# Three weight transfers issued ahead of the first rows, three more put into one run, on the queue of a state-space and LSTM kernel

## The reference, cut to what matters

```
x  = r                                   # (8 batches, 2048 steps, 512 features)
h  = layernorm(x)
y  = gelu(causal_conv(h, K) + D * h)     # K: one kernel of 2048 taps per feature, from a state-space model
x  = x + layernorm(y)
u  = layernorm(x)                        # what the LSTM-like cell reads
c0 = in_c for each of the 2048 positions
for each batch b, in order:              # u[b] is (2048 positions, 512)
    f = sigmoid(u[b] @ wf.T + c @ uf.T + bf)
    i = sigmoid(u[b] @ wi.T + c @ ui.T + bi)
    g = tanh   (u[b] @ wc.T + c @ uc.T + bc)
    c = f * c + i * g
h   = tanh(u @ wo.T + c_final @ uo.T + bo)
out = x + layernorm(h)
```

## Time and profile before

| | |
|---|---|
| median of three runs | 2647.38 us (2645.84 to 2648.0) |
| span of the profiled execution, first to last instruction | 2645.3 us |
| mean granted TensorE clock over the span | 0.983 |
| TensorE busy | 2527.1 us, 96% |
| VectorE, ScalarE, GpSimd busy | 1839.7, 1621.4, 1124.1 us |
| one core's HBM traffic | 292.88 MB read, 180.88 MB written |

### The profile page before, as it was taken

The page is one execution under the profiler, slowest core; times in us unless marked ns, Lnnn a source line. Parts: engine busy times, 40 slices in busy tenths (PEclk is TensorE's granted clock), DMA queues, the critical chain, the costliest instruction groups (busy, mean ns, idle before and its releaser), DMA issues.

```text
span 2645.3 us, 57571 instructions
## 1 busy us (share of the span) xinstructions
PE 2527.1 (96%) x22659; PEld 2205.2 (83%) x22659; DVE 1839.7 (70%) x3415; ACT 1621.4 (61%) x3003; POOL 1124.1 (42%) x1433
## 2 busy tenths in 40 slices
PE   5499999997899999999999999999999999999998
PEld 4278888886788888888888888888888888888887
DVE  7855556547887677776777887777677774467667
ACT  8657667566655555555556665555555554378777
POOL 7768687725332123222224342222222320067667
PEclk9799999998999999999999999999999999999999
DMA  8779797889774455445665755544556432489998
GB/s 348 294 227 310 266 316 268 272 292 335 195 196 116 125 141 164 127 116 125 146 161 153 193 162 142 162 130 116 124 142 159 131 85 49 156 337 347 369 360 347
DMA packets 507551, 542.52 MB, mean 205 GB/s; under 512 B 273936, under 2 KB 412944, under 8 KB 488720
## 3 DMA queue, kind: packets, MB, share of 16 engines
q1 hardware_dynamic: 507280, 538.85, 65.5%
HBM read 292.88 MB, written 180.88 MB: 179 GB/s over the span
## 4 chain that ended last, share of the span: by engine, by line
PE 84%; DVE 4%; POOL 4%; ACT 4%; DMA 2%; issue 2%; SPq 1%; DVEq 0%; POOLq 0%; ACTq 0%
PE bank L2150 31%; PE bank L2160 29%; PE bank L2206 8%; PE bank L2039 4%; PE bank L1989 3%; PE bank L2025 3%; PE bank L2047 2%; PE bank L2001 2%; PE bank L2181 2%; DVE big L1831 1%; PE bank L2009 1%; POOL big L890 1%; ACT big L1345 1%; POOL big L994 1%; DVE big L1888 1%
## 5 line engine op out<-in xcount | busy, mean ns | idle before, releaser
L2150 PE MATMUL bank<-big 128*128 128x256 f16 x8064 | 1081.2, 274 | 18.6 <-ACT big L1391 8.0
L2160 PE MATMUL bank<-big 128*128 128x256 f16 x7056 | 962.4, 273 | 0.0
L2150 PEld LDWEIGHTS bank<-big 128*128 128x128 f16 x8064 | 791.6, 98 | 116.4 <-ACT big L1391 9.7
L2160 PEld LDWEIGHTS bank<-big 128*128 128x128 f16 x7056 | 690.4, 98 | 79.9
L1035 POOL TENSOR_SCALAR big<-big 128x1 f32<-128x1 f32 x253 | 107.7, 426 | 1092.3 <-DVE big L1678 810.1
L1888 DVE TENSOR_TENSOR big<-bank,big 128x512 f32<-128x512 f32 x256 | 174.8, 683 | 196.9 <-PE bank L2160 193.8
L2206 PE MATMUL bank<-big 128*128 128x256 f16 x2688 | 295.3, 273 | 4.4 <-ACT bank L1325 4.0
L1301 ACT ACTIVATE big<-big 128x512 f32<-128x512 f32 x384 | 289.6, 803 | 14.0 <-DVE big L1888 11.9
L2206 PEld LDWEIGHTS bank<-big 128*128 128x128 f16 x2688 | 262.4, 98 | 36.9 <-ACT bank L1325 4.9
L1874 DVE TENSOR_TENSOR big<-bank,big 128x512 f32<-128x512 f32 x256 | 176.1, 688 | 142.8 <-PE bank L2160 119.1
L1233 ACT ACTIVATE big<-big 128x512 f32<-128x512 f32 x256 | 205.9, 808 | 104.4 <-POOL big L1037 101.1
(11 more groups left out here) (234 smaller groups left out, 3712.1 us busy)
## 6 DMA issues: line engine op xcount, KB each, us to landing
xtd<-big SPq DMA_DIRECT2D x60, 1024.0 KB, 6.9
big<-xr SPq DMA_DIRECT2D x16, 2048.0 KB, 9.1
big<-xg SPq DMA_DIRECT2D x64, 512.0 KB, 7.6
big<-kpad SPq DMA_DIRECT2D x32, 1024.0 KB, 12.1
yd<-big SPq DMA_DIRECT2D x16, 2048.0 KB, 16.8
big<-x SPq DMA_DIRECT2D x128, 256.0 KB, 3.3
x1d<-big SPq DMA_DIRECT2D x128, 256.0 KB, 3.2
big<-x1d SPq DMA_DIRECT2D x64, 512.0 KB, 8.8
```

What stands on the lines that cost most here:

```text
L2150: ins = e.matmul(o, WX[2 * g + lw][:, q, kt, 128 * a:128 * a + 128], slot[u % 2][:, part, lx, k0 + kt, :], start=(first and kt == 0 and (l ...
L2160: ins = e.matmul(o, WC[2 * g + lw][:, q, kt, 128 * a:128 * a + 128], cc[unit(u)[1] % 2][:, qc, lx, kt, :], start=False, stop=end, skip_gro ...
```

## The change

The definition of `load_y` is moved up unchanged, so that it can be called from the loop over turns. In turn i = NG, the last, SyncE now issues `load_y(0)`, waits for the four loads of WX[0..3] to have landed, and issues WX[4], WX[5] and WC[0]. From its old places `load_y(0)` with its wait, these three loads, and the later loads of WC[3], WC[4] and WC[5] are taken out; the last three now stand behind WC[1]. Nothing else is changed, and on no other engine is an instruction added, removed or moved.

```
                 if i == NG - 1:
                     ...
+                if i == NG:
+                    w.wait_ge(s["cv"], G * (NG - 1))
+                    load_y(0)
+                    w.wait_ge(s["wx"], 16 * 4)
+                    load_WX(4)
+                    load_WX(5)
+                    load_WC(0)
...
                     turn(8 * v + 1)
-                    load_WC(3)
                     store_x1(v, 3)
-                    load_WC(4)
...
                     store_xt(0)
-                    load_WC(5)
                     w.wait_ge(s["xs0"], 16)
                     w.wait_ge(s["xs1"], 16)
...
-            w.wait_ge(s["cv"], G * (NG - 1))
-            load_y(0)
             for c in CHUNKS[:2]:
                 load_x1(0, c)
...
-            w.wait_ge(s["wx"], 16 * 4)
-            load_WX(4)
-            load_WX(5)
             w.wait_ge(s["w_lo"], low_base(8))
             w.wait_ge(s["wd"], stored(7))
             w.wait_ge(s["fb"], 12)
-            load_WC(0)
             load_WC(1)
+            load_WC(3)
+            load_WC(4)
+            load_WC(5)
 
             w.wait_ge(s["fb"], 20)
             load_WC(2)
```

More of the change, by code:

```diff
@@ L600, in load_WC, with load_y @@
                 e.dma_start(WC[n].rearrange("p q k f -> p q (k f)"), wg[2 * g + 1][:, l]).then_inc(s["wc"], 16)
+            def load_y(v):
+                b, j = unit(v)
+                src = yd[:, :, b, 4 * j:4 * j + 4, :].rearrange("g t k h -> t g k h")
+                if v == 0:
+                    w.wait_ge(s["y0"], 16 * 7)
+                    w.wait_ge(s["y1"], 16 * 7)
+                    e.dma_start(yt[:, 0:NG - 2], src[:, 0:NG - 2]).then_inc(s["yl"], 16)
+                    return
+                w.wait_ge(s["y0"], 16 * 8)
+                w.wait_ge(s["y1"], 16 * 8)
+                if v == 1:
+                    w.wait_ge(s["yc"], 2)
+                elif v == 2:
+                    w.wait_ge(s["x1"], 4)
+                    w.wait_ge(s["yl"], 32)
+                else:
+                    w.wait_ge(s["ss"], 8 * v)
+                    w.wait_ge(s["xh"], 8 * v - 2)
+                    w.wait_ge(s["xlo"], 8 * v - 2)
+                e.dma_start(rows_y(v), src).then_inc(s["yl"], 16)
             e.dma_start(sm, small).then_inc(s["sm"], 16)
```

20 lines of the change are left out of this document (removed).

## The result

The changed kernel takes 2651.02 us (median of 20 runs, 2648.29 to 2652.72), the kernel before 2646.63 us (20 runs, 2645.09 to 2648.82). That is +4.4 us; the ratio is 1.0017, 95% interval [1.0011, 1.0023]. The forecast was 2650.7 us, or +3.3 over a kernel before of 2647.38; with 20 runs the kernel before is 0.75 us lower, so the forecast is 0.3 us off as a time and 1.1 us off as a change. The profiled execution took 2650.75 us, its span is 2649.1 us, 3.8 us more than before, at a mean granted clock of 0.982 (0.983 before).

What follows compares the result with a forecast made beforehand. The bound was TensorE, busy 96%, behind a start-up chain at 585 to 692 us whose delays reach the end one to one. 0.0 + 4.4 - 0.0 - 1.1 = +3.3 us gave 2650.7 us, range 2645.0 to 2655.0.

Steps and rivals of the forecast that it cites:

- Part 1: `load_y(0)` in the last turn: same place in SyncE's order, behind the store to `wd`; no gain, no cost, 0.0 us.
- Part 2: WX[4], WX[5], WC[0] ahead of the x chunks: transfers behind land 6.6 us later, unit 1's transposes 4.4 us later.
- no drop of its clock: TensorE in unit 0, no longer waiting 2.17 us for WX, was to keep its full clock, regaining 1.5 us.
- what VectorE gives back for it: VectorE's waits for TensorE in group 2, 0.63 + 1.27 = 1.9 us, were to close, leaving 4.7 of 6.6 us.
- the later gap: VectorE's 0.90 us wait for ScalarE before unit 1's low parts; 0.3 us of it was taken off.
- VectorE decides: Before unit 1, TensorE ends 2.3 us late and VectorE 6.6, so VectorE's delay sets the shift.
- Part 3: WC[3], WC[4] out of unit 1's preparation, lightening the queue near 640 us; taken as 0, at most 0.5 us.
- Part 4: WC[5] out from between stores of turned units: unit 2's x1 chunk lands earlier; 1.1 us gained, ends 0 and 2.2.
- Rival 1: At unit 1's rows, nothing is given back and the 6.6 us stay whole: 2654.0 us; chance 0.20.
- Rival 2: At the boundary, early weights cost nothing and the gains alone remain, together 5.9 us: 2641.5 us; chance 0.09.
- Rival 3: Delay mostly absorbed before unit 1, another chain into the transposes being last; some 3 us less, about 2647.7 us; chance 0.19.
- Rival 4: The change doesn't do what its words say; true of `load_y(0)`, already in the sum at 0; no chance given.

Runs made afterwards that it cites:

- e1: Changed kernel with WC[3], WC[4], WC[5] at their old places, so only the early loads; 2652.05 us, +5.3 over the kernel before.
- e3: Changed kernel with WX[4], WX[5], WC[0] behind the x chunks and `fbs`, ahead of the store of group 15; 2650.18 us, +3.4 over before.
- e4: Kernel before with only WX[4] loaded earlier, in turn NG - 1 just before the store to `wd`; 2646.19 us, -0.6.
- e5: Kernel before with only WC[5] moved behind the four x1 stores of unit 2; 2644.79 us, -0.9.
- e9: Kernel before with WC[3], WC[4] moved behind the first two x loads of unit 3 in unit 2's preparation; 2649.36 us, +3.4.
- e6: Kernel before with WC[3], WC[4], WC[5] moved behind the x1 stores of unit 2; 2648.05 us, +2.4.
- e7: Kernel before with the 1 MB store to `wd` moved from ahead of unit 0's rows to behind WX[5]; 2645.89 us, +0.3.
- e11: Changed kernel with the store to `wd` moved behind the x loads of unit 1; 2650.61 us, +4.7 over the kernel before.
- e2: Kernel before with WC[3], WC[4], WC[5] behind WC[1], the early loads at their old places; 2652.47 us, +5.7.
- e8: Kernel before with the store to `wd` behind WX[5] and WC[5] behind the x1 stores of unit 2; 2644.93 us, -0.7.
- e10: Kernel before with `wd` store behind WX[5], WC[5] behind unit 2's x1 stores, WC[3], WC[4] behind unit 3's first two x loads; 2650.20 us, +4.3.
- e12: Repeat of e8's kernel, measured again against the kernel before; 2645.12 us, -0.8.

## Why the prediction held, and where it did not

**Part 1, `load_y(0)`, 0.0 us.** Right: L608 at 585.49 instead of 585.25, landing for VectorE's L1664 at 593.90, foretold near 594.

**Part 2, the queue shift, 6.6 us.** Right in kind, mis-sized. The rows of unit 1 are +5.1 late in the changed kernel, +5.5 in e1 and +5.7 in e3, `fbs` +5.1 and +5.9. I had said that there is no hole in the queue and divided by 414 GB/s. The share of 0.97 over 25 us leaves 0.75 us, and from 596 to 608 the queue before moved more than I had taken:

```profile
596.00:608.00 12.00, 7.32 (x32) 6.55 (x32) 9.81 (x26) 7.86 (x12) 7.22 (x19) 0.57 1.02 424
```

2.75 MB at 424 GB/s are 6.5 us, less 0.75 is 5.7, which is the upper of the measured values; the spread to 5.1 is within what traces of one program differ by (-1.4 to +0.2 above). In the changed kernel all that was issued from 585.49 to 593.59 landed in the order of issue, as forecast. The Trainium skill allows a later descriptor to finish first ("DMA: Bandwidth & Descriptors", section "Queues, rings and completion order"); the landings of the changed kernel show no case of it.

**Part 2, "TensorE ... has no wait for WX any more ... and no drop of its clock", and what VectorE gives back for it, 1.9 us.** This is the step that failed. Counted from the gelu, VectorE's first L1875 is +5.1 late and its last row of group 2, L1889, +5.3: nothing was given back, the two waits stayed. I had let TensorE run up to 4.3 us ahead of VectorE's shift. In the changed kernel it can't, since ScalarE frees the bank of group 2 only behind gates that wait for VectorE; TensorE met 3.09 us there, and then worked at a clock of 0.57 for 4 us, so that it handed VectorE the products of group 2 as late as ever. "A clock of 1.00 from 620 on" is the one sign of the prediction that did not come.

The bank alone does not explain it. The columns: TensorE's last idle spell before the products of group 2, in us; the granted clock in the two windows of 2 us behind it; VectorE's two waits for TensorE in group 2; its last row of group 2, counted as above.

```
                      idle           clock        waits        end of group 2
before                2.17 WX[5]     0.63 0.51    0.63 1.27    39.15
changed kernel        3.09 bank      0.64 0.51    0.87 1.27    +5.31
e1_early_only         2.92 bank      0.54 0.61    0.86 1.27    +5.77
e4_wx4_in_gap         2.52 bank      0.50 0.77    0.61 1.27    +0.30
e5_wc5_late           2.46 WX[5]     0.60 0.54    0.73 1.27    -0.04
e9_wc34_in_gap        2.85 WX[5]     0.65 0.50    0.73 1.27    +0.46
e3_behind_fbs         0.95 bank      1.00 1.00    0.00 0.56    +4.23
e6_wc345_late         1.59 WX[5]     1.00 1.00    0.00 0.80    -2.59
e7_wd_late            0.69 bank      1.00 1.00    0.00 0.56    -3.47
e11_changed_wd_late   2.56 bank      1.00 1.00    0.00 0.56    -1.50
```

e2, e8, e10 and e12 are like the last four rows (1.00, waits of 0.56 to 0.61 together). Wherever the clock fell, the two waits are 1.9 us or more together; wherever it did not, 0.6 to 0.8. e3 has rows as late as the changed kernel's and the full clock there: 1.4 us come back between the rows (+5.7) and the end of group 2 (+4.2), and unit 1 begins at +3.7. So the give-back that was forecast is there when the clock holds, and the changed kernel did not get it. Between the rows of unit 1 (+5.1) and TensorE's unit 1 (+4.7) only 0.4 us came back, where 2.2 were forecast with the 0.3 for the later gap. The two errors, 1.5 too much for the shift and 1.8 too much given back, nearly cancel: 4.4 was forecast for unit 1 and 4.7 measured. That it came so near is luck.

**The place, "VectorE decides".** Right for the changed kernel, with a second chain close behind that I hadn't checked. Two chains come to unit 1: rows of unit 1 to VectorE (+5.1), and x1 stores of unit 1 to GpSimd's first half sums (+5.2). That they are equally late is no accident, since the stores wait for VectorE's sums of these rows: the first leaves SyncE at 627.19, when VectorE's L1686 ends, 621.88 before. But either can hold unit 1 alone. e11 takes the delay out of the rows and leaves the stores late by the queue, e2 has late stores and rows on time, and they start unit 1 at +4.9 and +5.2, with ScalarE waiting for the half sums. The sentence that "the x1 stores behind it see the same queue as before, shifted" was true, and it was this shift that I never followed further.

**Part 3, WC[3], WC[4] out of unit 1's preparation, 0.0 us.** Right with the rows at their old time or later: e9 has both loads out, with its rows at +0.2, and is at +0.1 at unit 1. With the rows early they may be worth about 1.2 us (e10 against e8, one trace each, less than traces of one program differ by), above my end of 0.5.

**Part 4, WC[5], -1.1 us.** Right in the traces: GpSimd's wait for the x1 chunk of unit 2 is 6.96 us before, 5.77 in the changed kernel, 7.87 with WC[5] put back (e1). From unit 1 to the first state product the changed kernel makes up 1.1 us. By medians it is 0.9, 0.9 and 1.0 the three times that it was asked (changed kernel against e1, where WC[3] and WC[4] move too; e5 against before; e8 against e7), each within the noise of the runs. So it is shown by the wait and consistent with the times, not shown by them.

**Rivals.** Rival 1 (nothing given back, +6.6) was right that nothing is given back before unit 1, though not on why, and wrong on its price: the shift itself is 5.1, and WC[5] was worth about 1. Its chance of 0.20 looks low: nothing in the earlier trace rows said that the waits would close, only that they were there. Rival 2 (early weights cost nothing) fell by the runs that have all three (changed kernel, e1, e3). Rival 3 (absorbed before unit 1, a second chain last) was right that the 7.1 us wait for the transposes is a join of several chains, and wrong that this would save time: the second chain starts from the first and was as late. Rival 4 was true of `load_y(0)`.

**What stays open.** The gaps between traces and medians are mostly accounted for. The traced execution of the kernel before took 2647.38 us, 1.7 us more than the kernel before beside e8 (median 2645.64), and e8's last gelu stands 0.8 us later than before's: together as much as the gap of 2.3. Of the 3.6 us in e10, 1.3 lie behind the first product with a state, and its profiled execution (2648.07) was 2.1 below its median. So a trace of e5 to e12 looks up to 1.7 us better against the kernel before than the kernel is. Why e6 gains 2.7 us at unit 1 and e5 nothing, with rows of unit 1 as early in the one (-1.4) as in the other (-1.3), is in the table of the clock: both end group 2 there already, e6 at -2.6, e5 at 0.0, and e5's clock had fallen. What decides whether the clock falls stays open: behind 2.52 us of idling it did (e4), behind 2.56 us at the same bank it did not (e11). That the clock, and no other difference of these kernels, keeps VectorE's waits is read from the 14 traces and was not varied by itself. A version with early rows, WC[5] late and WC[3], WC[4] away from all transposes was not tried.

## What to carry to other kernels

Before moving a load forward on a full queue, divide its bytes by the queue's rate and add that to every transfer behind it; then follow each of these, not only the first, to the place where they join. A wait that is to be "given back" or removed is worth something only if the engine that it holds is free to run ahead: look in the timeline of the engine that empties its buffers for the next thing it would stand for, and do not count on the clock that it would have without the wait. And where a load hurts is decided by what stands directly behind it on the issuing engine: WC[3] and WC[4] cost nothing that shows among the transposes of unit 1 while the rows are not early, and 3.4 us directly ahead of four of unit 2 (e9).

## What the runs showed of the hardware that I had not expected

- Issuing itself takes longer behind a full queue. One x1 store of 256 KB took SyncE 3.29 us to issue behind five weight loads, 10.48 us behind eight (e2). Four DMA transposes took 8.95 us to issue, and 12.43 us behind two weight loads of 896 KB (e9).
- The granted clock did not follow the wait that was removed. Behind 2.17 us for a load it was 0.63 and 0.51 in the two windows of 2 us; with that wait gone, 0.64 and 0.51 behind 3.09 us for ScalarE. And it is not bound to such a spell either: behind 2.56 us at the same bank it stayed 1.00 (e11).

```profile
628.00:630.00 2.00, 1.60 (x15) 1.44 (x16) 1.93 (x5) 2.00 (x5) 0.22 (x1) 1.00 1.04 423
```
